# Mixture-of-experts layer: the activation is turned by a transposing DMA instead of TensorE and ScalarE, and weight chunks are loaded two to a tile

## The reference, cut to what matters

```python
x = x + xattn(layernorm(x), ctx, Wq, bq, Wk, bk)     # 4 x 1024 rows of 1024
h = layernorm(x)                                      # 4096 rows
logits = h @ gate_w.T + gate_b                        # 32 experts, each row goes to its best 4
w = softmax(top4(logits))
# for each (row, expert) pair, rows sorted by expert:
gate = min(h @ w_gate[e] + b_gate[e], 7);  up = clip(h @ w_up[e] + b_up[e], -7, 7)   # 1024 -> 512
activated = (up + 1) * gate * sigmoid(1.702 * gate)   # 512 values a row
out = activated @ w_down[e] + b_down[e]               # 512 -> 1024
x = x + sum over the row's 4 experts of w * out
```

## Time and profile before

| | |
|---|---|
| median of 3 runs | 3280.85 us (3279.0 to 3282.75) |
| the profiled execution | 3284.01 us, span 3282.2 us |
| PE busy | 3120.8 us, 95% of the span |
| DVE, ACT, POOL busy | 52%, 39%, 18% |
| granted TensorE clock, mean | 0.973 of full speed |
| DMA | 468.03 MB, 143 GB/s over the span; the queue of SP 27.2% of 16 engines, the queue of POOL 22.2% |

### The profile page before, as it was taken

How to read it: one execution, slowest core, us unless ns; L and a number is a source line. 1 busy time by engine, 2 the same in 40 slices (tenths; PEclk the granted TensorE clock), 3 DMA queues, 4 the chain that set the end, 5 groups by cost and what they waited for, 6 DMA issues and landing times.

```text
span 3282.2 us, 46620 instructions
## 1 busy us (share of the span) xinstructions
PE 3120.8 (95%) x15456; PEld 1609.9 (49%) x15457; DVE 1720.9 (52%) x2851; ACT 1280.6 (39%) x1299; POOL 595.1 (18%) x502
## 2 busy tenths in 40 slices
PE   6799899995999999999999999999999999999997
PEld 3455555553455444455455444544555445455553
DVE  4576767774453544554544545444455444454432
ACT  3553434422342434443433434344344333343421
POOL 0023323322111111111111111111111111111111
PEclk8899999997999999999999999999999999999999
DMA  4123222354564555556555655655565655555432
GB/s 149 64 104 124 103 84 104 104 166 146 144 171 117 148 154 154 174 159 198 155 155 150 173 154 166 192 173 144 142 171 164 197 156 153 154 163 144 110 63 58
DMA packets 210439, 468.03 MB, mean 143 GB/s; under 512 B 57761, under 2 KB 57761, under 8 KB 210114
## 3 DMA queue, kind: packets, MB, share of 16 engines
q1 hardware_dynamic: 164514, 314.84, 27.2%
q0 software_dynamic: 45856, 152.33, 22.2%
HBM read 354.64 MB, written 112.46 MB: 142 GB/s over the span
## 4 chain that ended last, share of the span: by engine, by line
PE 71%; DMA 3%; SPq 1%; issue 1%; ACT 0%; DVE 0%; POOL 0%; ACTq 0%; POOLq 0%; DVEq 0%
PE psG L1167 22%; PE psU L1167 22%; PE psY L1189 22%; PE psX L1173 4%; PE psA L1180 2%; DMA bias<-in_L_ffn_b_down 2%; DMA idxg<-slots 0%; SPq L959 0%; DMA idxs<-slots 0%; SPq L112 0%; DMA acc<-y,idxs 0%; SPq L962 0%; DMA xg<-xn_tab,idxg 0%; ACT aT L1057 0%; DVE gt L1122 0%
## 5 line engine op out<-in xcount | busy, mean ns | idle before, releaser
L1189 PE MATMUL psY<-W,aT 128*128 128x512 f16 x3456 | 777.9, 382 | 23.1 <-ACT aT L1057 23.1
L1167 PE MATMUL psG<-W,xT 128*128 128x512 f16 x3456 | 772.4, 380 | 2.9 <-ACT xT L1053 2.9
L1167 PE MATMUL psU<-W,xT 128*128 128x512 f16 x3456 | 769.4, 379 | 0.0
L1167 PEld LDWEIGHTS psG<-W,xT 128*128 128x128 f16 x3456 | 338.8, 98 | 413.0 <-issue 6.1
L1189 PEld LDWEIGHTS psY<-W,aT 128*128 128x128 f16 x3456 | 339.7, 98 | 406.2 <-ACT aT L1057 24.5
L1167 PEld LDWEIGHTS psU<-W,xT 128*128 128x128 f16 x3456 | 338.2, 98 | 375.6
L1114 DVE SCALAR_TENSOR_TENSOR y<-bias,idxs,y 128x1024 f32<-128x1024 f32 x144 | 185.0, 1284 | 544.7 <-ACT y L1064 544.7
L123 DVE SCALAR_TENSOR_TENSOR W<-stage,W 128x2048 f16<-128x2048 f32 x192 | 438.7, 2285 | 4.8 <-ACT W L118 4.8
L1021 POOL DMA_INDIRECT acc<-y,idxs x144 | 227.4, 1579 | 1011.9 <-DVE y L1114 996.3
L1064 ACT ACTIVATE y<-psY,idxs 128x1024 f32<-128x1024 f32 x144 | 160.5, 1114 | 604.6 <-DMA idxs<-slots 577.9
L118 ACT ACTIVATE W<-stage 128x2048 f16<-128x2048 f32 x192 | 365.1, 1902 | 10.8 <-issue 5.5
(11 more groups left out here) (136 smaller groups left out, 2305.1 us busy)
## 6 DMA issues: line engine op xcount, KB each, us to landing
stage<-in_L_ffn_w_gate SPq DMA_DIRECT2D x64, 1024.0 KB
stage<-in_L_ffn_w_up SPq DMA_DIRECT2D x64, 1024.0 KB
stage<-in_L_ffn_w_down SPq DMA_DIRECT2D x64, 1024.0 KB
stage<-in_x SPq DMA_DIRECT2D x32, 512.0 KB
xr<-in_x SPq DMA_DIRECT2D x32, 512.0 KB
acc<-xr SPq DMA_DIRECT2D x32, 512.0 KB
xn_tab<-x2h SPq DMA_DIRECT2D x32, 512.0 KB
bias<-in_L_ffn_b_down SPq DMA_DIRECT2D x32, 512.0 KB, 13.6
```

The costliest lines, as they stand in the source:

```text
L1167: op = pe.matmul(ps[:], xT[:, k, :, a], weights(par, c, offset + k * I, I), start=k == 0 and n == 0, stop=k == KH - 1 and n == 2)
L1189: op = pe.matmul(psY[:, h * HALF:(h + 1) * HALF], aT[:, k, :, a], weights(par, c, 2 * KH * I + k * H + h * HALF, HALF), start=k == 0 and n ...
```

## The change

In each step of the expert phase the four transposes on PE, the readout on ACT and the PSUM tensor psA go. `ahl` is laid out with all HI parts and then all LO parts, 1024 fp16 in a row of a partition; SP issues one transposing DMA from SBUF to SBUF for each tile, which writes `aT` as eight blocks of 128 by 128. SP does so at the start of the next tile's step, after the load of gather indices and before its wait for `s_added`; it waits for the LO part (`s_alo`) and for the down product before (`s_Y`), since `aT` is a single buffer. PE's down product waits for the DMA (`s_aT`), and ACT waits for it before it overwrites `ahl`. `s_Y` starts at 1, hence the changed counts. The chunks are loaded two behind each tile of the first three; the first phase loads one chunk less.

```diff
-                    if b1 is None:
+                    if b1 is None and s < NT - 1:
                         sp.wait_ge(s_wlo, s - 1)
                         g["load_chunk"](sp, 0, s - 2 + RING)
...
-    LOAD = [[3, 4], [5], [6, 7, 8]]
+    LOAD = [[2, 3], [4, 5], [6, 7]]
...
-        ahl = sb("ahl", [P, I, 2], F16)
-        aT = sb("aT", [P, KI, P, 2], F16)
+        ahl = sb("ahl", [P, 2, I], F16)
+        aT = sb("aT", [P, 2 * KI, P], F16)
...
-        psA = psum("psA", [P, KI * P], F32)
...
+            def transpose_act(i):
+
+                alone(sp, s_alo, i + 1, s_past)
+                alone(sp, s_Y, i + 1, s_past)
+                sp.dma_start_transpose(out=aT[:, :, :], in_=ahl[:].rearrange("p a i -> p (a i)")).then_inc(s_aT, 16)
+
             def step(i, e, j, more, prev_guard):
 
                 sp.wait_ge(s_xg, 16 * i + 32)
                 load_slots(sp, idxg, i + 2, s_idxg)
 
                 def prev():
+                    transpose_act(i - 1)
                     alone(sp, s_added, i, s_past)
                     load_slots(sp, idxs, i - 1, s_idxs)
...
-            def evac_a(i):
-                act.wait_ge(s_A, i + 1)
-                act.activation(aT[:].rearrange("p k q a -> p (k q a)").bitcast(F32), psA[:], ACT.Copy).then_inc(s_aTev, 1)
-
...
-                guarded(act, prev_guard, lambda: evac_a(i - 1))
                 if j is not None:
                     guarded(act, more, lambda: cut_one(1))
                 evac_x(i + 1)
+                guarded(act, prev_guard, lambda: alone(act, s_aT, 16 * i, s_past))
                 act.wait_ge(s_act, i + 1)
-                act.activation(ahl[:, :, HI], av[:], ACT.Copy, scale=S_ACT).then_inc(s_ahi, 1)
+                act.activation(ahl[:, HI, :], av[:], ACT.Copy, scale=S_ACT).then_inc(s_ahi, 1)
...
-            def transpose_act(i):
-                pe.wait_ge(s_ahi, i + 1)
-                pe.wait_ge(s_alo, i + 1)
-                for n in range(KI):
-                    op = pe.transpose(psA[:, n * P:(n + 1) * P], ahl_w[:, n * P:(n + 1) * P], ident[:])
-                op.then_inc(s_A, 1)
-
             def down(i, par):
-                pe.wait_ge(s_aTev, i + 1)
+                alone(pe, s_aT, 16 * i + 16, s_past)
...
-                            op = pe.matmul(psY[:, h * HALF:(h + 1) * HALF], aT[:, k, :, a],
+                            op = pe.matmul(psY[:, h * HALF:(h + 1) * HALF], aT[:, a * KI + k, :],
...
-                def between():
-                    transpose_act(i - 1)
-                    pe.wait_ge(s_uread, i)
-                guarded(pe, prev_guard, between)
+                guarded(pe, prev_guard, lambda: alone(pe, s_uread, i, s_past))
```

More of the change, by code:

```diff
@@ L912, in experts @@
         av = sb("av", [P, I], F32)
-        ahl = sb("ahl", [P, I, 2], F16)
-        aT = sb("aT", [P, KI, P, 2], F16)
+        ahl = sb("ahl", [P, 2, I], F16)
+        aT = sb("aT", [P, 2 * KI, P], F16)
         y = sb("y", [P, H], F32)
         xg_w = xg[:, :].bitcast(F32)
-        ahl_w = ahl[:, :, :].rearrange("p i a -> p (i a)").bitcast(F32)
         psG = psum("psG", [P, HALF], F32)
@@ L933, in experts @@
         s_X = sem("x_transposed")
-        s_A = sem("act_transposed")
         s_Y = sem("down_done")
@@ L945, in experts @@
         s_xTev = sem("xT_evacuated")
-        s_aTev = sem("aT_evacuated")
+        s_aT = sem("act_transposed")
         s_y0 = sem("y_weighted")
@@ L1007, in _ @@
             tt = start_of(sp, E)
+            transpose_act(tt - 1)
             alone(sp, s_added, tt, s_past)
@@ L1062, in weigh_y @@
                 act.wait_ge(s_added, i + 1)
-                act.wait_ge(s_Y, i + 1)
+                act.wait_ge(s_Y, i + 2)
                 act.activation(y[:], psY[:], ACT.Copy, scale=idxs[:, 2:3].bitcast(F32)).then_inc(s_y0, 1)
@@ L1079, in cut_one @@
                     if c == 2 * PER_W:
-                        act.wait_ge(s_Y, t0 + 1)
+                        act.wait_ge(s_Y, t0 + 2)
                     cut_hi(act, e + 1, 1 - par, c)
@@ L1105, in _ @@
             tt = start_of(act, E)
-            evac_a(tt - 1)
             weigh_y(tt - 1)
@@ L1142, in step @@
                 dve.wait_ge(s_ahi, i + 1)
-                dve.scalar_tensor_tensor(out=ahl[:, :, LO], in0=av[:], scalar=S_ACT, in1=ahl[:, :, HI],
+                dve.scalar_tensor_tensor(out=ahl[:, LO, :], in0=av[:], scalar=S_ACT, in1=ahl[:, HI, :],
                                          op0=ALU.mult, op1=ALU.subtract).then_inc(s_alo, 1)
@@ L1213, in step @@
                 weights_cut(3 * PER_W)
+            pe.sem_inc(s_Y, 1)
             pe.wait_ge(s_xg, 16)
@@ L1224, in _ @@
             tt = start_of(pe, E)
-            transpose_act(tt - 1)
             down(tt - 1, 1)
```

## The result

The changed kernel takes 3440.49 us, the median of 4 runs (3413.97 to 3447.22), against 3280.43 us (3279.0 to 3282.75) of the kernel before on the same chip: a ratio of 1.047, 95% interval 1.042 to 1.053. It is slower by 160 us; I had forecast 3191 and a range up to 3365. Times in this document are medians without disturbed runs (one run of 5184 us at a granted clock of 0.591, of the kernel of experiment 11, is left out). The profiled execution has a span of 3441.2 us at a mean granted clock of 0.948.

A forecast was written before the change was run, and what follows sets the result against it. PE, busy 95% of the span, was taken to bound the kernel: 3284.0 - 62.9 (transposes) - 29.8 (bias stalls) + 3 (late DMA) = 3194.3 us, 3191 as median. The range was 3178 to 3365 us.

The forecast's parts named there:

- The transposes go: PE's chain in each tile step: psA's four transposes vanish, 0.44 us a step, 143 x 0.44 = 62.9 us gained.
- The four bias stalls go: PE's down product no longer waits for an `aT` readout behind a bias-bound sigmoid: 29.8 us gained, slow clock included.
- Queue empty at S + 8.1, the scatter's bytes from S + 8.8: SP's queue at an expert's end: two chunks and biases through at S + 8.1, POOL's scatter moving from S + 8.8.
- S: Start of a tile's gate product on PE; the prediction wanted `aT` at S + 11.23.
- T: The transposing DMA's own time on the engines: taken as 1.05 us, landing at S + 10.9, 0.3 us before PE wants it.
- Beyond 0.7 us each part of T is stretched by 1 / 0.375 = 2.7: At an expert's end SP's queue gets only 37.5% of the engines for the scatter's 4 us, stretching the DMA's remainder.
- The clock, 0 to 2.1 us an end: In rival 3, slow clock after PE idles costs 0 to 2.1 us at each of 31 ends, 0 to 65 us.
- POOL's wait for `idxg` gets shorter by 3 to 5 us: Sign at an expert's end: POOL's wait for its index load shrinks by 3 to 5 us.
- Rival 3: Transposing DMA slow in the queue, T = 3.5 us: PE idles 4.1 us at 31 ends, 3315 to 3380 us; chance 0.18.
- Rival 1: Scatter's bytes go first at experts' ends: PE idles 2 to 2.5 us at 31 ends, 3250 to 3266 us; chance 0.20.
- The check that I had named, waits above 93 us: Sign: if the down product's waits for the transposing DMA sum to over 93 us, the change loses.

The follow-up runs named there:

- experiment 11: Kernel before (transposes on PE and ACT) with the new chunk loading order and the biases ahead of the chunks: 3246.35 us, ratio 0.989.
- experiment 3: Kernel before with the new order of chunk loads alone, transposes still on PE and ACT: 3257.81 us, ratio 0.992.
- experiment 1: Changed kernel with POOL's scatter held back until the next tile's transposing DMA has landed: 3378.63 us, ratio 1.029.
- experiment 12: Bare expert's-end queue, last transfer transposing or plain copy (256-byte or 2 KB rows): beside scatter-add 18.1 to 20.1, 15.9 to 16.4, 14.6 to 15.7 us.
- experiment 4: Bare sequence, four transposing DMAs with or without another queue's transfer: alone 7.5 us, scatter-add alone 6.0 to 6.2, both together 10.4.
- experiment 13: Changed kernel with a plain copy in 256-byte rows in place of the transposing DMA, turning left out: 3278.7 us, ratio 0.998.
- experiment 9: Bare expert's-end queue, sweep of scatter-add delays (2 to 5 DVE memsets): 16.4 to 16.9, 15.4 to 16.3, 17.9 to 20.2, 15.0 to 18.3 us.
- experiment 14: Changed kernel with a plain copy of whole 2 KB rows in place of the transposing DMA, turning left out: 3250.57 us, ratio 0.992.
- experiment 8: Changed kernel with the old order of loads, three chunks ahead of the biases and the transposing DMA: 3409.42 us, ratio 1.040.
- experiment 2: Changed kernel with each tile's transposing DMA issued at the end of its own SP step, ahead of the biases: 3207.6 us, ratio 0.979.

## Why the prediction was wrong

- *The transposes go, 0.44 us a step.* Right: 16.41 us in the chain.
- *The four bias stalls go.* Right in that PE waits for no bias any more. But 23 of the 29.8 us are had by the new order of loads alone (experiment 3).
- *Queue empty at S + 8.1, the scatter's bytes from S + 8.8.* Right at the end shown: 369 GB/s to S + 7.8, and the scatter's first packets lie between S + 8.8 and S + 9.3.
- *T, the DMA's own time: taken 1.05 us, between 0.7 and 9.2.* Measured 1.4 us alone (0.70 x 2) and about 1.7 us at the clean end of experiment 1. By the prediction's own formula 1.6 us is (1.6 − 0.7) x 2.7 + 1.2 behind S + 8.8, S + 12.4, or 1.2 us late at the prediction's 31 ends: 37 us, a result near 3225. A small miss that did not decide the sign.
- *Beyond 0.7 us each part of T is stretched by 1 / 0.375 = 2.7.* This is the step that failed. The 37.5% of the earlier trace rows was the share of a load with large packets beside a scatter. I carried a share of bytes over to a transfer of another kind. What the runs show in its place: about a third of the DMA goes at once, and the rest is through only with the scatter. The two hold each other up so that both take several us more than the sum of their work: at the end shown the scatter needed 11 us for what it does in 4 to 5 alone, and from 1991 to 2000 the engines were busy 69% (38.2 for the scatter's queue, 30.6 for SP's) with work in both queues. PE wanted the operand at S + 11.2 and got it 6.4 us late on average at 30 ends.
- *The clock, 0 to 2.1 us an end.* Right in size, at its upper edge: 55 to 65 us over 30 ends, 1.8 to 2.2 us each.
- *POOL's wait for `idxg` gets shorter by 3 to 5 us.* It did not: 276.2 us in 27 waits is 10.2 us each, against 10.4 before. This index load stands ahead of the transposing DMA in the queue, and POOL gets it only at 1999.91, S + 18.7. So more than the one DMA was held up.
- *The rivals.* Rival 3 had the outcome, waits past 93 us with the clock on top, but for a wrong reason: it made the DMA slow by itself and decided from T of 2.4 us. T was 1.6 and the kernel still lost. Rival 1, the scatter ahead, was false in its order and right that the scatter is the partner to fear. None of the rivals let the time of two transfers together exceed the sum of their work; rival 3 so ended at 3380, and the range at 3365. The check that I had named, waits above 93 us, did tell: 188.7.

The Trainium skill's "Advanced Engine Details and Errata", X-Bar Transpose (TRN2), says that transposing DMAs are as fast as regular ones. Alone it is nearly so here against a copy in equal packets, 13.1 to 13.5 us against 12.4 to 13.2 in experiment 12 (12.2 to 12.6 with 2 KB packets); beside an accumulating scatter it is not, 18.1 to 20.1 against 15.9 to 16.4. The same section says that transposes in flight from two queues mix up wavefronts of 16 rows. If one transposing DMA moves forward in such steps across all engines, an engine held by a scatter's packet would hold up the others; that would suit packets that are under way three to four times as long and engines that idle with work left. No run here shows it, and the mechanism stays open, as does why one delay of the sweep cost up to 3 us more than its neighbours, and why the pairs of experiment 4 lost nothing.

## What to carry to other kernels

Put a DMA that an engine will wait for ahead of bulk loads in its queue, so that it is over before a scatter of another queue starts to move bytes; moving one issue was worth 233 us here, almost six times the 39.7 us that the transposing DMA gains where nothing collides. A share of DMA time read from one pair of transfers holds for that pair's packet sizes and kinds, not for another's; where a new kind of transfer (a transposing one) is added, price it in the worst company that it will meet, and let that price exceed the sum of the work. Try the separate edits separately: the loading order was a gain of its own and the changed kernel hid it.

## What the runs showed of the hardware that was not expected

- *Issuing a transposing DMA into a full queue holds SP.* In the changed kernel the issue takes 1.27 us where the queue is idle (first row below) and 7.15 us at the expert's end shown above; in the kernel of experiment 13 a plain copy at such an end takes SP 0.65 us (second). A scatter issued meanwhile seems to lengthen it: in the bare sequence behind the same loads it is 3.55 to 4.33 us without POOL (experiment 12) and 7.25 to 7.77 us with the scatter at a delay of 2 (experiment 9). What stands behind it on SP must wait as long.

```profile
2010.22 1.27 SPq L973 DMA_TRANSPOSE aT<-ahl  x1
```

```profile
2005.12 0.65 SPq L973 DMA_DIRECT2D aT<-ahl  x1
```

- *How long PE may idle before the clock falls is no single number.* In the changed kernel an idle 3.08 us kept it and one of 2.59 us (at 2533.48) lost it; in the kernel of experiment 14 an idle 2.43 us lost it. The granted clock over the matmuls behind them is 1.00, 0.75 and 0.74:

```profile
2224.40 5.34 PE L1182 MATMUL psY<-W,aT 128*128 128x512 f16 x24 [3.08 <-DMA aT<-ahl]
```

```profile
1989.41 7.03 PE L1182 MATMUL psY<-W,aT 128*128 128x512 f16 x24 [2.43 <-DMA aT<-ahl]
```

- *The changed kernel spreads more from run to run*: 33 us over 4 runs, against 12 us over 13 runs of the kernel before. The collision alone does not explain it: the kernel of experiment 8 collides at every end and spreads 6 us, that of experiment 2 hardly collides and spreads 23 us.
